# New instruction orders ahead of the first scan, and three steps moved inside the pairs, of a bidirectional mamba mixer on one Trainium2 core

## The reference, cut to what matters

```python
x = x + gb * _L0_ffn_ref(h, ...)                 # two expert outputs per token are summed, gated, added
h = _layernorm(x, axis=-1) * (1 + ca) + sa
# _L1_attn_ref(h): layernorm with ln1, then _mamba forward and on the reversed sequence
xz = jnp.einsum('ble,ie->bli', x, in_w); xc, z = jnp.split(xz, 2, axis=-1)
xc = _silu(conv1d(xc) + conv_b)                  # 4 taps, causal
dt, Bm, Cm = jnp.split(jnp.einsum('bld,rd->blr', xc, xproj_w), [DTR, DTR + DS], axis=-1)
dt = jax.nn.softplus(jnp.einsum('blr,dr->bld', dt, dt_w) + dt_b)
dA = jnp.exp(dt[..., None] * A); dBx = dt[..., None] * Bm[:, :, None, :] * xc[..., None]
# h_t = dA_t * h_{t-1} + dBx_t for each of DS = 16 states and 256 channels; y_t = sum_s h_t * C_t
y = (y + xc * D) * _silu(z)
```

## Time and profile before

| | |
|---|---|
| median of three runs | 3324.89 us (3307.72, 3324.89, 3325.00) |
| the profiled execution: its own time | 3343.91 us |
| its span, first to last instruction | 3342.0 us |
| the hand-written stage, 1238.5 to 1356.5 us | 118 us |
| first to last forward scan | 1356.5 to 2954.0 us, 256 scans |
| TensorE's granted clock, mean over the span | 0.907 of full speed |

### The profile page before, as it was taken

How to read it: one execution, slowest core, us unless ns; L and a number is a source line. 1 busy time by engine, 2 the same in 40 slices (tenths; PEclk the granted TensorE clock), 3 DMA queues, 4 the chain that set the end, 5 groups by cost and what they waited for, 6 DMA issues and landing times. The chain is left out here.

```text
span 3342.0 us, 55577 instructions
## 1 busy us (share of the span) xinstructions
PE 2743.4 (82%) x18699; PEld 2103.7 (63%) x18699; DVE 2508.6 (75%) x3291; ACT 2260.4 (68%) x4086; POOL 2148.2 (64%) x1488
## 2 busy tenths in 40 slices
PE   6999999320999986788888888888888888769984
PEld 3555555220899972566666666666666666669983
DVE  5788887442333334799999999999999999977993
ACT  2777777420222225989999998999999999756652
POOL 2233332365333325989999898999999999843564
PEclk6999999555999988989999999999999999889996
DMA  5555554211665665222222222222222222322322
GB/s 136 97 100 103 103 101 78 74 55 59 193 196 190 193 170 166 81 73 78 78 74 75 81 81 76 81 74 75 80 78 77 83 73 76 107 57 66 86 58 67
DMA packets 202783, 321.54 MB, mean 96 GB/s; under 512 B 37418, under 2 KB 109638, under 8 KB 197898
## 3 DMA queue, kind: packets, MB, share of 16 engines
q1 hardware_dynamic: 189282, 299.01, 32.4%
q0 software_dynamic: 12224, 18.29, 1.6%
q10 hardware_dynamic: 1008, 0.72, 0.1%
HBM read 269.84 MB, written 55.68 MB: 97 GB/s over the span
## 5 line engine op out<-in xcount | busy, mean ns | idle before, releaser
L1701 POOL TENSOR_TENSOR resid_x<-s_ux,s_B_rows 128x1024 f32<-128x1024 f32 x256 | 606.2, 2368 | 122.1 <-PE s_y L2422 120.9
L2253 DVE TENSOR_TENSOR_SCAN resid_x<-s_dA,resid_x 128x1024 f32<-128x1024 f32 x256 | 582.0, 2274 | 51.8 <-ACT s_dA L1913 49.7
L2261 DVE TENSOR_TENSOR_SCAN resid_x<-s_late,s_back_in 128x1024 f32<-128x1024 f32 x256 | 583.7, 2280 | 4.7 <-PE s_back_in L2409 2.3
L2422 PE MATMUL s_y<-identity,resid_x 128*128 128x128 f32 x4096 | 559.1, 282 | 6.6 <-issue 3.4
L2422 PEld LDWEIGHTS s_y<-identity,resid_x 128*128 128x128 f32 x4096 | 498.9, 146 | 59.2 <-issue 32.2
L1709 POOL TENSOR_TENSOR resid_x<-resid_x,s_C_rows 128x1024 f32<-128x1024 f32 x192 | 454.7, 2368 | 1.8 <-DVE resid_x L2253 1.8
L2268 DVE TENSOR_TENSOR resid_x<-resid_x,s_C 128x1024 f32<-128x1024 f32 x320 | 382.8, 1196 | 30.8 <-PE s_C L2397 30.8
L566 DVE TENSOR_REDUCE a_row_max<-a_maxscores 128x2 f32<-128x512 f32 x512 | 336.0, 684 | 80.2 <-PE a_maxscores L632 79.7
L2409 PE MATMUL s_back_in<-identity,resid_x 128*128 128x128 f32 x2048 | 297.5, 292 | 101.7 <-ACT resid_x L1934 51.8
L1913 ACT ACTIVATE s_dA<-s_dt,s_A 128x510 f32<-128x510 f32 x512 | 330.2, 677 | 73.8 <-DVE resid_x L2253 72.4
L1923 ACT ACTIVATE s_late<-s_dt,s_A 128x510 f32<-128x510 f32 x512 | 338.2, 710 | 0.0
(11 more groups left out here) (459 smaller groups left out, 5577.1 us busy)
## 6 DMA issues: line engine op xcount, KB each, us to landing
s_B_rows<-forward_rows SPq DMA_DIRECT2D x256, 256.0 KB, 3.2
e_w<-L_ffn_w_by_expert SPq DMA_DIRECT2D x71, 768.0 KB, 4.7
s_C_rows<-forward_rows SPq DMA_DIRECT2D x192, 256.0 KB, 3.2
a_Q<-split_qk SPq DMA_DIRECT2D x96, 192.0 KB
split_qk<-a_parts SPq DMA_DIRECT2D x32, 384.0 KB, 2.8
e_x<-slot_inputs SPq DMA_DIRECT2D x71, 130.0 KB
a_K<-split_qk SPq DMA_DIRECT2D x64, 128.0 KB
s_late<-choice_outputs SPq DMA_DIRECT2D x16, 512.0 KB, 4.5
```

The lines of the kernel that those rows point to most:

```text
L1701: tt(R[s, 0], ux[par][:], brow[s % BRING][:].unsqueeze(1).broadcast_to([P, C2, W]), ALU.mult).then_inc(S["in_ready"], 1)
L2253: nc.vector.tensor_tensor_scan(r, a, r, 0.0, ALU.mult, ALU.add).then_inc(S["scanned"], 1)
L2261: nc.vector.tensor_tensor_scan(r[:, ::-1], a[:, ::-1], b[:, ::-1], 0.0, ALU.mult, ALU.add).then_inc(S["scanned"], 1)
L2422: last = mm(YP[:, t, c2 * P:(c2 + 1) * P], R[s, d][:, c2, t * P:(t + 1) * P], core.ident[:], is_transpose=True, start=((s, d) == (0, 1) an ...
```

## The change

It changes orders only: no instruction is added or taken away, and all sizes and buffers stay. (1) The stage ahead of the first scan gets a new order on GpSimd, ScalarE, VectorE and TensorE; in it the decays of state 1 of pair 0 are also issued ahead of `silu(1, 1)`, and are left out of the loop. (2) In chunk 22 the conv of the next pair stands behind the decays of state 12, not ahead of them. (3) In chunk 17 the forward row of C of state 9 stands ahead of the next pair's `conv(0,1)`, not behind it. The parts of the loop:

```diff
+ROWS_AHEAD = (18,)
...
-                            if c in ACT_BETWEEN:
+                            if c in ACT_BETWEEN and s != SHUT:
                                 between(i, u, c)
-                            if s + 1 < DS and live(i, 1):
+                            if s + 1 < DS and live(i, 1) and not (isinstance(i, int) and i + s == 1):
                                 decays(i - 1, (u + 1) % 2, s + 1)
                             if s + 1 == DS and live(i, 0):
                                 decays(i, u, 0)
+                            if c in ACT_BETWEEN and s == SHUT:
+                                between(i, u, c)
...
-                            if live(i, 1):
+                            if live(i, 1) and c not in ROWS_AHEAD:
                                 c_rows(i - 1, (u + 1) % 2, s, 0 if s in OWN else 1)
...
+                        if c + 1 in ROWS_AHEAD and live(i, 1):
+                            c_rows(i - 1, (u + 1) % 2, s + 1, 0 if s + 1 in OWN else 1)
                         if live(i, 0):
                             for what in PE_AT.get(c, ()):
                                 prep(i, u, what)
```

The orders of the stage, GpSimd, ScalarE, VectorE and TensorE in this order:

```diff
                 x_variance(1)
+                h_variance(0)
                 x_offset(1)
-                h_variance(0)
                 h_offset(0)
                 x_add(3)
                 x_add(4)
                 x_variance(2)
+                x_offset(2)
                 x_add(5)
-                x_offset(2)
                 shift(1)
                 x_variance(3)
                 shift(2)
                 x_offset(3)
+                shift(3)
                 x_add(6)
-                shift(3)
                 less_exp(0, 0, 0)
                 less_off(0, 0, 0)
+                x_add(7)
                 step_size(0, 0, 0, 0)
-                x_add(7)
-                shift(4)
+                times_x(0, 0, 0, 0)
+                x_variance(4)
                 less_exp(0, 0, 1)
                 less_off(0, 0, 1)
+                x_offset(4)
                 step_size(0, 0, 0, 1)
-                x_variance(4)
-                times_x(0, 0, 0, 0)
-                x_offset(4)
+                shift(4)
                 times_x(0, 0, 0, 1)
...
-                rows(1, 0)
                 h_root(0)
                 normed(0, 0)
                 normed(0, 1)
+                rows(1, 0)
+                turned(0)
                 rows(1, 1)
-                turned(0)
...
+                rows(3, 0)
                 conv(0, 0, 1, 0)
                 x_root(3)
-                rows(3, 0)
+                rows(3, 1)
                 conv(0, 0, 1, 1)
                 silu(0, 0)
                 nc.scalar.preload_act_table_set(EXP_TABLE)
-                rows(3, 1)
+                rows(4, 0)
...
                 prep(0, 0, ("part2",))
                 back_input(0, 0, 1)
+                h_root(1)
+                decays(0, 0, 1)
+                back_decays(0, 0, 1)
                 silu(1, 1)
...
                 h_stats(0)
+                x_stats(2)
                 gate(4)
-                x_stats(2)
                 x_stats(3)
+                scale(1)
                 gate(5)
-                scale(1)
                 x_stats(4)
+                h_stats(1)
                 x_stats(5)
-                h_stats(1)
                 scale(2)
                 h_stats(2)
+                scale(3)
                 gate(6)
-                scale(3)
...
                 sums(3)
+                sums(4)
                 turned(0)
                 pe.wait_ge(N["taps_kept"], 2)
                 products(0, 0, "conv", 0, 0)
+                sums(5)
                 products(0, 0, "conv", 0, 1)
-                sums(4)
                 products(0, 0, "conv", 1, 0)
                 products(0, 0, "conv", 1, 1)
-                sums(5)
                 sums(6)
                 products(0, 0, "dt", 0, 0)
                 products(0, 0, "dt", 0, 1)
+                prep(0, 0, ("z", 0))
                 sums(7)
                 products(0, 0, "dt", 1, 0)
-                prep(0, 0, ("z", 0))
                 prep(0, 0, ("z", 1))
```

More of the change, by code:

```diff
@@ L2134, in _ @@
                 ln_off(0, 0, 0)
-                rows(4, 0)
+                rows(4, 1)
                 pre_step(0, 0, 0, 1)
-                rows(4, 1)
                 gate(0, 0, 0)
+                rows(5, 0)
                 exp_plus1(0, 0, 1)
+                ln_off(0, 0, 1)
                 gate(0, 0, 1)
-                ln_off(0, 0, 1)
                 turned(1)
                 pre_step(0, 0, 1, 0)
-                rows(5, 0)
+                rows(5, 1)
+                x_root(4)
                 prep(0, 0, ("bc",))
-                rows(5, 1)
                 exp_plus1(0, 1, 0)
-                x_root(4)
                 prep(0, 0, ("bT",))
                 ln_off(0, 1, 0)
+                prep(0, 0, ("part0",))
+                pre_step(0, 0, 1, 1)
                 rows(6, 0)
-                pre_step(0, 0, 1, 1)
                 rows(6, 1)
                 exp_plus1(0, 1, 1)
-                prep(0, 0, ("part0",))
                 ln_off(0, 1, 1)
@@ L2159, in _ @@
                 rows(7, 1)
+                prep(0, 0, ("part1",))
                 conv(1, 1, 0, 1)
-                prep(0, 0, ("part1",))
                 prep(0, 0, ("uT", 0))
@@ L2169, in _ @@
                 conv(1, 1, 1, 1)
-                h_root(1)
                 prep(0, 0, ("part2",))
                 back_input(0, 0, 1)
+                h_root(1)
+                decays(0, 0, 1)
+                back_decays(0, 0, 1)
                 silu(1, 1)
@@ L2305, in _ @@
                 h_stats(0)
+                x_stats(2)
                 gate(4)
-                x_stats(2)
                 x_stats(3)
+                scale(1)
                 gate(5)
-                scale(1)
                 x_stats(4)
+                h_stats(1)
                 x_stats(5)
-                h_stats(1)
                 scale(2)
                 h_stats(2)
+                scale(3)
                 gate(6)
-                scale(3)
+                h_stats(3)
                 x_stats(6)
-                h_stats(3)
                 gate(7)
@@ L2612, in _ @@
                 products(0, 0, "dt", 0, 1)
+                prep(0, 0, ("z", 0))
                 sums(7)
                 products(0, 0, "dt", 1, 0)
-                prep(0, 0, ("z", 0))
                 prep(0, 0, ("z", 1))
-                products(0, 0, "dt", 1, 1)
                 pe.wait_ge(S["z_read"], 1)
                 turned(1)
+                products(0, 0, "dt", 1, 1)
                 products(0, 0, "bc", 0)
@@ L2626, in _ @@
                 prep(0, 0, ("uT", 0))
+                prep(0, 0, ("uT", 1))
                 products(1, 1, "conv", 1, 1)
-                prep(0, 0, ("uT", 1))
                 turn_input(0, 0)
```

## The result

| | before | after |
|---|---|---|
| median, 18 runs each | 3314.48 us | 3291.96 us |
| profiled execution, span | 3342.0 us | 3281.8 us |
| VectorE's first step of the stage | 1238.58 us | 1211.92 us |
| first forward scan, from there | 117.88 us | 104.99 us |
| third forward scan, from there | 137.85 us | 125.40 us |

The ratio of after to before is 0.9919, with a 95% interval of [0.9901, 0.9937]. (The two medians of the table are 22.5 us apart, a ratio of 0.9932, which lies within it.) On the median of 3324.9 us from which the prediction started, that is 26.9 us less, against 28 predicted.

What follows compares the result with a forecast made beforehand. The pairs were taken to go by VectorE, 94% busy, with TensorE's full stretch bounding part of each. Terms of 16.8 + 0 + 11.2 = 28 us off the median of 3324.9 gave 3297 us, range 3282 to 3316.

Steps and rivals of the forecast that it cites:

- Step 2: Pairs, chunk 22: decays of state 12 ahead of the conv, 1.2 us a pair, 16.8 us over 14 pairs.
- Two signs: VectorE in a pair: next to no wait at scan 12, about 1.5 us at scan 13.
- Step 3: Pairs, chunk 17: row of C ahead of `conv(0,1)`; the 2.03 us stall goes, priced at 0.
- The 1.5 us forecast at the backward weighing: VectorE, state 9: waits 1.5 us for the second row of C, which can't come earlier.
- Rival (e): Pairs: the row of C ahead of `conv(0,1)` waits and the kernel gets slower, 3342 us; 5%.
- Step 1: Stage ahead of the first scan: new order, first scan 11.6 us earlier, third scan and stage 11.2 us.
- the two readings of conv(0,0): Stage, TensorE: at full clock the sum is 28 us; at the low clock conv(0,0) ends 2.9 us later, 25.
- rival (c): Stage gives nothing through an unseen wait, such as `h_offset(1)` behind late `h_root(1)`: 3308 us; 7%.
- the 0.4 us worked out for it: Cost of state 1's decays ahead of `silu(1,1)`, worked through with the wait of `part2` for GpSimd.
- rival (a): Both gains come as summed, stage 7 to 13 us, pairs 12 to 20: 3292 to 3306 us; 68%.

Runs made afterwards that it cites:

- The kernel that is shortest in the trace and not by time: Kernel before with step 2, `sums(4)` and `sums(5)` moved, `conv(1,1)` ahead of chunk 21's adding up and `normed` in chunk 17: ratio 0.9896.
- the kernel at 0.9879: Changed kernel with `conv(1,1)`'s product ahead of the adding up in chunk 21 and `normed` in chunk 17, not 21: ratio 0.9879, median 3274.71 us.

## Why the prediction was right

**Step 2** was worked out as 1.2 us a pair, 16.8 in all: the decays fit into ScalarE's wait for the last product, the table load behind comes 1.2 us earlier, and half of the stall at scan 12 reappears at scan 13. Alone it gave 1.2 us a pair and 17.2 in all. Two signs were off by little in after: scan 12 keeps 0.36 us, which belongs to step 3 (both kernels with step 2 and without step 3 have no wait there); and scan 13 waits 1.60, not 1.5. Neither changes the sum: pairs are 1.2 us shorter with step 3 and without it.

**Step 3** was priced at nothing, because the second row of C can't come earlier, and the step alone and the change without it both measured nothing. The 1.5 us forecast at the backward weighing are 1.55. Rival (e), a row of C that waits, didn't come: TensorE starts it at 1975.02 with no wait ahead.

**Step 1** was worked out as 11.6 us at the first scan and 11.2 at the third. The profiled before overstates its own stage: TensorE's first sum in it took 4.16 us, 3.70 in after. In three other executions of the old order, one of them with a single move in it, the first scan came at 115.75, 115.93 and 117.81 (that sum took 3.70, 3.70 and 4.11 us). The mean of the four is 116.84, that of six executions of the new stage 105.11: 11.7 us. The term held. The choice between the two readings of conv(0,0) was right: 3.68 us, so 28 and not 25. It had some luck: I had worked out waits of 2.2 and 1.2 us around the four small matmuls, and they were 1.76 and 1.65. In the kernels with the order of the sums alone they were 2.15 and 1.65, and conv(0,0) took 5.37 us.

Behind the sum two sizes were off and in part cancelled. The last residual add came 72.6 us into the stage where my working has 75.0 (1.2 of it is the lucky start, 1.3 the working: two `dt` products and half of `z` took 5.8 us, not 6.8). And GpSimd needed 32.4 us from there to the first scan where I had 31.2: TensorE's `bc` products, which took 3.65 us in before, ran at the low clock, and `less_exp` waited 1.35 us for it. The wait for `h_root(1)` that rival (c) names is there on GpSimd, 2.89 us, and the second scan then waits 3.98:

```profile
1323.21 0.30 POOL L1676 TENSOR_TENSOR neg_mean_rstd<-ln_mean,rstd 128x56 f32<-128x56 f32 x1 [2.89 <-ACT rstd L1886]
...
1325.92 2.29 DVE L2258 TENSOR_TENSOR_SCAN resid_x<-s_dA,resid_x 128x1024 f32<-128x1024 f32 x1 [3.98 <-POOL resid_x L1702]
1333.19 1.22 DVE L2273 TENSOR_TENSOR resid_x<-resid_x,s_C 128x1024 f32<-128x1024 f32 x1 [4.98 <-PE s_C L2402]
```

At the third scan it cost the 0.4 us worked out for it: that scan came 12.5 us earlier in the two profiles and the first 12.9.

What I had not seen is how step 1's gain is made. I walked through the whole new order and gave its sum to the order as a whole. Two moved sums account for all of it, and the other moves together cost some 3 us. The sum was right; a reader who took from it that each move helps would be wrong. A slip in the prediction's own numbers: its rival (a) spans 3292 to 3306, and further down the same case is given as 3288 to 3306; 3292 follows from its terms.

The traces also show where the 31 us ahead of the stage come from. In the profiled before TensorE waited 63.5 us, in ten waits, at its own instruction issue between 640 and 840 us; in none of the other twelve traces has it one such wait there. And in the three others in which the stage began late (1219.7 to 1227.0 us) its clock had fallen sooner: from 560 to 600 us it was 0.50 to 0.66, and 0.96 in the trace in which the stage began at 1207.3. The kernel that is shortest in the trace and not by time is a matter of the clock too: of its six executions two had a mean clock of 0.918 or more and took 3263 and 3271 us, one of these being the profiled one, and four had 0.913 or 0.914 and took 3285 to 3289. Of the kernel at 0.9879 five of six were at 0.917 or more. What stays open is why the clock falls sooner in one execution of the same kernel than in another, and what held up the issue.

## What to carry to other kernels

Price a moved step by what is late next behind it: a wait of 2.17 us was worth 1.2, because ScalarE's table load behind it came only 1.2 us sooner, and one of 2.03 was worth nothing, because TensorE had the same full stretch ahead of the next row. In an order that waits across engines, look for the one step that the longest waits lead back to and move that alone first; the rest of a large reordering may be paying it back. And where two profiled executions differ, split the difference by landmarks before giving any of it to the change: here 26.7 of 60.2 us lay ahead of the first changed instruction.

## What the hardware showed

Orders that are nearly alike got another clock from the chip. In the stage, `turned(0)` (four small matmuls, 0.66 us) and conv(0,0) follow `sums(4)`. In the six executions of the new stage TensorE had waited 1.76 or 1.77 us ahead of `turned(0)` and conv(0,0) took 3.68 us; in the three with the order of `sums` alone it had waited 2.13 to 2.15 there, with the same 1.65 (or 1.64) behind, and conv(0,0) took 5.37. `bc` took 3.65 us after a wait of 1.22 in before, 5.24 to 5.33 after 2.19, and 5.00 to 6.64 after 3.15. The wait straight ahead doesn't settle it alone: the transposes of state 1 took 1.94 us in one execution and 1.06 in another after the same 1.02, and `bc` spreads from 5.00 to 6.64 us after the same 3.15.
The Trainium skill, "TensorE: Matmul & The Clock Gate", section "What's actually happening", says that the gate follows how busy the array has recently been; the rows of `turned(0)` and `bc` agree, and so does the run in which five extra matmuls kept `bc` at 3.65 us.
